# Unread matrix products in a recurrence's first turns, zeroing moved to GpSimd, and experts' first chunks put ahead of the gates' transposes

## The chip, the cores and the metric

The kernel runs on one core of a Trainium2 chip. A core has five engines that run side by side and meet at semaphores: TensorE (PE: matrix products; PEld is its weight load), VectorE (DVE), ScalarE (ACT), GpSimd (POOL) and SyncE (SP, which here only starts transfers). TensorE's clock is granted at one of two levels, 1.2 or 2.4 GHz, which the profile shows as 0.50 and 1.00. The metric is the device time of the whole program in microseconds; less is better.

## The reference

A two-layer pre-norm decoder on x and ctx_1024, each 64 sequences x 64 tokens x 128 channels in float32:

```python
x = x + attn0(layernorm(x))            # 16 heads of 8, rotary, causal
x = x + mlstm(layernorm(x), ctx, ctx)  # 4 heads of 32, below
x = x + experts(layernorm(x))          # below
x = x + attn1(layernorm(x))            # 16 heads of 8, distance bias, causal
x = x + cross(ctx, layernorm(x))       # 8 heads of 64
x = x + soft_experts(layernorm(x))     # 64 experts x 32 slots

def mlstm(q, k, v):                    # the "recurrence", in its parallel form
    gates = concat(q, k, v) @ gate_kernels + biases      # input and forget gate of 4 heads
    cs = cumsum(log_sigmoid(fg))
    log_D = where(tril, cs - cs.T, -inf) + ig.T
    max_log_D = max(log_D, -1); D = exp(log_D - max_log_D)
    C = (q @ k.T) / sqrt(32) * D
    h = (C / (maximum(abs(sum(C)), exp(-max_log_D)) + 1e-6)) @ v
    return headwise_layernorm(h) * outnorm_scale

def experts(x):                        # 1 shared of 512, 15 routed of 256
    shared = gelu(x @ sW1 + sb1) @ sW2 + sb2
    weights = softmax(x @ gW + gb)
    gated = weights where among the top 3, else 0
    routed = gelu(x @ rW1[e] + rb1[e]) @ rW2[e] + rb2[e]  # all 15, weighted by gated
    return shared + sum(gated[e] * routed[e]) + x
```

## The kernel before

The 4096 tokens are 32 tiles of 128 (NT = 32, two sequences each). x stays in SBUF through all stages; each stage leaves the normalized, transposed x (g_xnT) for the next. The stages follow one another with a barrier between them: load and norm, attention 0 (tiles at_), the recurrence (ml_), the experts (ff_), attention 1 (at_ again), cross-attention (xa_), soft experts (sm_). In a stage each engine has its own instruction stream, written out by hand as turns; every wait is a semaphore count. An engine runs its stream strictly in this order, so what stands in it behind a wait waits too.

**Attention** (`attention`, both layers): vblk holds the values spread out so that one product serves two heads; the places between the values must be zero. DVE zeroes its four buffers (L493) at the start of its stream, each with an increment of `zeroed`. ACT waits for that when it first writes each buffer (L640). In layer 0 what follows on DVE is the rotation's first products (L544) from the projections of PE (L439); then SP turns pairs by DMA (L381), and POOL sums (L572, L575) and spreads the keys (L582). In layer 1 DVE copies the projections (L554, L555) and POOL spreads the keys (L582).

**Recurrence** (`mlstm`): the gates of all tokens come first, with chains of small steps between engines. PE projects and transposes them (L723 to L731), waits for DVE's and ACT's log-sigmoid, makes the cumulative sum (L735), transposes (L737), waits for the running minimum, transposes again (L739). Then 32 turns of one tile each. In a turn PE makes the outputs of tile t-2 (L757, bank p_h), transposes a finished tile (L300), makes the values of tile t (L770, bank p_n) and the decay and scores of tile t+1 (L782, L785, L792, bank p_x, two in turn). ACT takes exponentials (L945), copies the values (L956) and splits heads (L932); DVE multiplies (L851), and with POOL normalizes the outputs of earlier tiles. L782 of a tile waits for L851 of the tile two before.

**Experts** (`experts`): eight groups of 512 tokens, in each 34 chunks of 128 hidden units (4 of the shared expert, 2 of each routed one). A chunk: three products with W1 in split float32 (L1134 to L1136, bank p_h, two in turn), Gelu on ACT (L1306), for routed chunks the product with the gate on DVE (L1240), rounding on ACT (L1317), the rest on POOL (L1081), and four chunks later three products with W2 (L1121 to L1123). Turn t also prepares group t+1: logits (L1150) at chunk 1, a router of 16 steps on DVE from chunk 4 with an exponential on ACT at chunk 7 (L1320), the rounding of x (L1288, and the remainder on DVE, L1231) at chunk 20, transposes of the gates on PE (L1155) at chunk 21, and their copy on ACT (L1325). SP stores the copy and spreads each gate over 128 partitions (L1087, L1098, five buffers). Turn -1 has no chunks and prepares group 0 in the same order: logits, router, x, transposes. In turn 0 ACT also rounds the late weights at chunks 4, 8, 12, 16, 20 and 24 (L1277), and DVE makes their remainders (L1185). ACT must load a table when it goes between Gelu and the exponential.

The lines that set the places:

```python
AT_LOGITS, AT_ROUTER, AT_G_T = 1, 4, 21
AT_X = 20
SPLIT_AT = [4, 8, 12, 16, 20, 24]
```

## Time and profile before

| | us |
|---|---|
| median of 3 runs | 2082.07 |
| the three runs | 2078.18 to 2083.69 |
| profiled execution, its own time | 2085.51 |
| its span, first to last instruction | 2083.6 |
| mean granted TensorE clock over the span | 0.965 |

All rows come from the one profiled execution. "L735" is a line of the kernel. A row of the timeline gives start, duration, engine, line, operation, the tile written <- the tiles read, the shape; in square brackets the idle time of the engine before it and who released it. A row of windows gives busy time of each engine in a stretch; its number after POOL is the granted clock. In the turns of the recurrence PE works without a pause at the low clock, then at the high one with short waits. Attention 0 lasts from about 50 to 256 us, the recurrence from 257 to 386 us, the experts from 387 to 842 us, attention 1 from there to about 1045 us.

### The profile page before, as it was taken

The page shows a single profiled execution, that of the slowest core. Times are in us where ns is not written, and L with a number is a line of the kernel's source. Part 1 is how long each engine was busy: PE and PEld are TensorE (multiplying, and loading weights), DVE is VectorE, ACT ScalarE, POOL GpSimd, SP SyncE. Part 2 cuts the span into 40 slices and gives each one's busy share as a digit, 9 for nine tenths or more (in the row PEclk, how much of TensorE's full clock was granted, in tenths as well). Part 3 has the DMA queues.
Part 4 walks back from the last instruction along what each step waited for, and adds up shares of the span by engine and source line. Part 5 has one row for each costly group of instructions (what it writes and reads, how often), then busy time and mean ns, then how long its engine had stood idle before and what let it go on. Part 6 is the DMA issues. An engine that isn't in the chain of part 4 may idle for free. (4 is left out here: it accounts for less than half of the span.)

```text
span 2083.6 us, 62428 instructions
## 1 busy us (share of the span) xinstructions
PE 1872.1 (90%) x23360; PEld 1479.8 (71%) x23422; DVE 1459.4 (70%) x3903; ACT 1449.4 (70%) x4203; POOL 1117.0 (54%) x1445
## 2 busy tenths in 40 slices
PE   5799798599999999799879999767999999999898
PEld 3566566477777777466668888646888888888787
DVE  7799748556666664577746666577777777777567
ACT  5588758488888888588858888666666666666542
POOL 5677427578888889455423333137544444445420
PEclk9999959799999999899989999998999999999999
DMA  3011010122222222000011111110000000000101
GB/s 97 27 46 41 13 32 3 48 91 72 72 77 77 77 72 66 23 2 2 2 26 33 34 34 34 47 39 4 5 15 18 6 15 5 15 15 3 55 8 39
DMA packets 60620, 72.48 MB, mean 35 GB/s; under 512 B 10264, under 2 KB 38696, under 8 KB 60064
## 3 DMA queue, kind: packets, MB, share of 16 engines
q1 hardware_dynamic: 51104, 64.29, 10.5%
q10 hardware_dynamic: 9216, 4.20, 0.7%
q8 instruction: 188, 3.08, 0.6%
q14 instruction: 112, 0.92, 0.1%
HBM read 51.43 MB, written 4.44 MB: 27 GB/s over the span
## 5 line engine op out<-in xcount | busy, mean ns | idle before, releaser
L1081 POOL TENSOR_TENSOR ff_hl<-ff_hid,ff_hh 128x512 fp32r<-128x512 f32 x272 | 349.5, 1302 | 74.5 <-ACT ff_hh L1317 65.7
L1935 POOL TENSOR_TENSOR sm_zsum<-sm_zsum,sm_logits 128x512 f32<-128x512 f32 x120 | 154.1, 1284 | 276.4 <-ACT sm_logits L1961 274.7
L1240 DVE TENSOR_TENSOR ff_hid<-ff_p_b,ff_gates 128x512 f32<-128x512 f32 x240 | 164.5, 686 | 150.0 <-ACT ff_p_b L1306 148.9
L1978 ACT ACTIVATE sm_sT<-sm_p_s 128x512 f32<-128x512 f32 x128 | 69.5, 594 | 220.8 <-PE sm_p_s L1771 220.8
L613 ACT ACTIVATE at_pr<-at_p_s,at_small 128x64 f32<-128x64 f32 x512 | 155.3, 330 | 62.7 <-DVE at_small L501 62.7
L1317 ACT ACTIVATE ff_hh<-ff_hid 128x512 fp32r<-128x512 f32 x272 | 169.9, 625 | 36.9 <-DVE ff_hid L1240 36.8
L1306 ACT ACTIVATE ff_p_b<-ff_p_h,early_b 128x512 f32<-128x512 f32 x240 | 157.0, 654 | 20.5 <-PE ff_p_h L1136 19.1
L1947 POOL TENSOR_TENSOR sm_logits<-sm_logits,sm_peak 128x512 f32<-128x512 f32 x128 | 163.1, 1295 | 13.6 <-ACT sm_comb L1996 12.9
L1785 PE MATMUL sm_p_l<-g_phi,g_xnT 128*128 128x256 f32 x512 | 143.3, 407 | 26.4 <-ACT sm_logits L2006 25.3
L582 POOL TENSOR_TENSOR at_kblk<-at_kT,early_heads 128x512 f32<-128x512 f32 x128 | 131.9, 1051 | 35.5 <-PE at_p_s L479 27.8
L1819 PE MATMUL sm_p_y<-sm_w,sm_sT 128*32 128x128 f32 x4096 | 125.4, 274 | 9.2 <-ACT sm_combT L1968 8.6
L1884 DVE TENSOR_REDUCE sm_rmax<-sm_p_l 128x2 f32<-128x512 f32 x128 | 88.3, 690 | 64.3 <-PE sm_p_l L1785 63.6
L1785 PEld LDWEIGHTS sm_p_l<-g_phi,g_xnT 128*128 128x128 f32 x512 | 91.6, 198 | 54.9 <-ACT sm_logits L2006 28.0
L1827 PE MATMUL sm_p_o<-sm_yy,sm_combT 128*64 128x129 f32 x2048 | 127.5, 276 | 1.5 <-issue 1.5
L1819 PE MATMUL sm_p_s<-sm_w,sm_sT 128*32 128x128 f32 x4096 | 124.3, 273 | 1.3 <-issue 1.3
L1819 PEld LDWEIGHTS sm_p_y<-sm_w,sm_sT 128*32 128x32 f32 x4096 | 107.6, 110 | 22.9 <-ACT sm_sT L1978 11.6
L1916 DVE TENSOR_TENSOR sm_yy<-sm_p_y,sm_wb 128x512 f32<-128x512 f32 x128 | 88.0, 691 | 50.1 <-PE sm_p_y L1819 50.1
L1134 PE MATMUL ff_p_h<-ff_xh,fw_w1h 128*128 128x512 f32 x272 | 113.8, 418 | 9.1 <-ACT ff_p_b L1306 9.0
L1827 PEld LDWEIGHTS sm_p_o<-sm_yy,sm_combT 128*64 128x64 f32 x2048 | 110.2, 136 | 15.8 <-DVE sm_yy L1916 12.5
L1585 ACT ACTIVATE xa_pr<-xa_p_s,xa_sm 128x128 f32<-128x128 f32 x256 | 91.8, 391 | 38.8 <-DVE xa_sm L1497 38.8
L281 POOL TENSOR_TENSOR xa_n_rstd<-xa_n_mv,g_eps 128x1 f32<-128x1 f32 x32 | 19.9, 620 | 177.2 <-DVE xa_n_mv L267 177.2
L1121 PE MATMUL ff_p_y<-ff_hh,fw_w2h 128*128 128x512 f32 x272 | 110.7, 407 | 4.6 <-POOL ff_hl L1081 2.4
(301 smaller groups left out, 5616.8 us busy)
## 6 DMA issues: line engine op xcount, KB each, us to landing
ff_gates<-kept_gates SPq DMA_DIRECT2D x120, 256.0 KB, 3.2
xa_kturn<-xa_ksin SPq DMA_DIRECT2D x128, 64.0 KB, 2.0
at_turned<-at_terms SPq DMA_DIRECT2D x64, 64.0 KB, 1.9
sm_w<-in_w_soft SPq DMA_DIRECT2D x8, 512.0 KB, 3.5
early_whole<-in_L_ffn_rW SPq DMA_DIRECT2D x30, 128.0 KB, 2.6
early_xs<-in_x ACTq DMA_DIRECT2D x32, 64.0 KB, 2.0
ld_ctx<-in_ctx ACTq DMA_DIRECT2D x32, 64.0 KB, 2.1
x_kept<-early_xs SPq DMA_DIRECT2D x1, 2048.0 KB, 7.4
```

What stands on the lines that cost most here:

```text
L582: op = pool.tensor_tensor(kblk[:, v % 2, b, :, :], row_bc(kT[:, v, b * S:(b + 1) * S], HH), col_bc(heads[:, :], S), ALU.mult)
L613: op = act.activation(pr[:, v, h * S:(h + 1) * S], p_s[0][:, h * S:(h + 1) * S], ACT.Exp, bias=small[:, v, 0, h:h + 1], accum_out=small[:, ...
L1081: eng.tensor_tensor(hl[:, q, :], hid[:, q, :], hh[:, q, :].bitcast(F32), ALU.subtract).then_inc(h_split, 1)
L1134: pe.matmul(p_h[n % PH][:, :], w1h[:, c, :], xh[:, u, :], start=True, stop=False)
L1240: dve.tensor_tensor(h, p_b[c % 2][:, :], gates[:, n % GR, :], ALU.mult).then_inc(scaled, 1)
L1306: act.activation(into, p_h[(NC_FF * t + c) % PH][:, :], ACT.Gelu, bias=b1[:, c:c + 1]).then_inc(gelud, 1)
L1317: act.activation(hh[:, q, :], hid[:, q, :], ACT.Copy).then_inc(h_rounded, 1)
L1785: mm = pe.matmul(p_l[h][:, a * CW:(a + 1) * CW], xnT[:, t * P:(t + 1) * P], phi[:, c % 2, :], start=True, stop=True)
L1819: mm = pe.matmul((p_y, p_s)[j % 2][a][SP * k:SP * (k + 1), (b * CQ + q) * D:(b * CQ + q + 1) * D], sT[:, j % 2, a, b, n_ * SP:(n_ + 1) * S ...
L1827: mm = pe.matmul(p_o[j % 2][b * S:(b + 1) * S, a * E1:a * E1 + D + 1], combT[:, j % RING_C, q, a, b * S:(b + 1) * S], yy[:, j % 2, a * PER ...
L1935: pool.tensor_tensor(z, z, logits[:, j % RING_L, :, :], ALU.add).then_inc(summed, 1)
L1947: pool.tensor_tensor(here, here, row_bc(peak[:, c % 2, :], TU), ALU.subtract).then_inc(centred, 1)
```

## The change

1. Attention (both layers): the four zeroings of vblk go from DVE to the head of POOL's stream.
2. Recurrence: PE makes products that nobody reads, identity times mask in bfloat16, 128x128 by 128x256 (`keep_busy`): 16 before the cumulative sum, 4 before the first transpose, 3 before the second; in turns 1 and 2 eight more at the head of the tile's values; in turns 1 to 11 four more behind the wait for the former tile's copied values. They write bank p_n, or bank p_h1 for the eights. In all 83.
3. Experts: turn -1 rounds x before the router. The transposes of group 0's gates and their copy stand behind chunk 2 of turn 0. In turn 0 what prepares group 1 (logits, router, exponential, transposes, gates' copy; not x) comes five chunks later (LATE = 5).

```diff
-            for v in range(R):
-                dve.memset(vblk[:, v, :, :, :], 0.0).then_inc(zeroed, 1)
...
         def _(pool):
+            for v in range(R):
+                pool.memset(vblk[:, v, :, :, :], 0.0).then_inc(zeroed, 1)
             at["in"].wait(pool)
...
+            def keep_busy(n, bank=p_n):
+                for _ in range(n):
+                    pe.matmul(bank[:, 0:W], identb[:, :], mask[:, :], start=True, stop=True)
+            keep_busy(16)
             pe.wait_ge(gate_step, 4)
...
+            keep_busy(4)
             pe.wait_ge(u_made, 3)
...
+            keep_busy(3)
             pe.wait_ge(max_made, 1)
...
+                    if 0 < k < 3:
+                        keep_busy(8, p_h[1])
                     if has(k - 1):
                         pe.wait_ge(v_copied, k)
+                    if 0 < k < 12:
+                        keep_busy(4)
...
-        AT_LOGITS, AT_ROUTER, AT_G_T = 1, 4, 21
+        AT_LOGITS, AT_ROUTER, AT_G_T, LATE = 1, 4, 21, 5
...
+                late = LATE if t == 0 else 0
...
-                    if c == AT_LOGITS and nxt:
+                    if c == AT_LOGITS + late and nxt:
...
-                    if c == AT_G_T and nxt:
-                        pe.wait_ge(r_step, STEPS * (t + 2))
+                    n = t if t == 0 and c == 2 else t + 1
+                    if live(n) and ((c == AT_G_T + late and t >= 0) or (n == 0 and t == 0)):
+                        pe.wait_ge(r_step, STEPS * (n + 1))
...
-                    if c == AT_X and nxt:
+                    if c == (AT_X if t >= 0 else AT_ROUTER) and nxt:
...
-                    if nxt and c >= AT_ROUTER and c - AT_ROUTER < len(router):
-                        router[c - AT_ROUTER]()
+                    if nxt and 0 <= c - AT_ROUTER - late < len(router):
+                        router[c - AT_ROUTER - late]()
...
-                    if c == 7 and nxt:
+                    if c == AT_ROUTER + 3 + late and nxt:
...
-                    if c == AT_G_T + 1 and nxt:
-                        act.wait_ge(gT_done, t + 2)
+                    n = t if t == 0 and c == 2 else t + 1
+                    if live(n) and ((c == AT_G_T + 1 + late and t >= 0) or (n == 0 and t == 0)):
+                        act.wait_ge(gT_done, n + 1)
```

PE's instructions in the recurrence, from the last transposes of the gates to the values of tile 1, before:

```order
L731 MATMUL ml_p_x<-g_ident,ml_gT 128x128 x8
L735 MATMUL ml_p_h<-ml_logf,mw_tri 128x128
L737 MATMUL ml_p_h<-g_ident,ml_nu 128x128
L739 MATMUL ml_p_h<-g_ident,ml_negM 128x128
L782 MATMUL ml_p_x<-mw_mask,mw_identb 128x256
L785 MATMUL ml_p_x<-ml_negM,ml_sel 64x64 x8
L792 MATMUL ml_p_x<-ml_q,early_ctxT 64x128 x4
L770 MATMUL ml_p_n<-mw_centre,early_ctxT 128x256
L782 MATMUL ml_p_x<-mw_mask,mw_identb 128x256
```

The same place after the change (L738 is `keep_busy`; the other lines have moved down by 7 to 13):

```order
L731 MATMUL ml_p_x<-g_ident,ml_gT 128x128 x8
L738 MATMUL ml_p_n<-mw_mask,mw_identb 128x256 x16
L742 MATMUL ml_p_h<-ml_logf,mw_tri 128x128
L738 MATMUL ml_p_n<-mw_mask,mw_identb 128x256 x4
L745 MATMUL ml_p_h<-g_ident,ml_nu 128x128
L738 MATMUL ml_p_n<-mw_mask,mw_identb 128x256 x3
L748 MATMUL ml_p_h<-g_ident,ml_negM 128x128
L795 MATMUL ml_p_x<-mw_mask,mw_identb 128x256
L798 MATMUL ml_p_x<-ml_negM,ml_sel 64x64 x8
L805 MATMUL ml_p_x<-ml_q,early_ctxT 64x128 x4
L783 MATMUL ml_p_n<-mw_centre,early_ctxT 128x256
L795 MATMUL ml_p_x<-mw_mask,mw_identb 128x256
```

Nothing else on PE changed its order here; the unread products stand before the three waits.

PE's instructions at the start of the experts, before (L1150 logits, L1155 transposes of the gates, L1134 to L1136 one chunk):

```order
L1150 MATMUL ff_p_q<-early_gw,g_xnT 128x15 x4
L1155 MATMUL ff_p_q<-g_ident,ff_sel 15x128 x4
L1134 MATMUL ff_p_h<-ff_xh,fw_w1h 128x512
L1135 MATMUL ff_p_h<-ff_xl,fw_w1h 128x512
L1136 MATMUL ff_p_h<-ff_xh,fw_w1l 128x512
```

And after (L1165 logits, L1149 to L1151 one chunk, L1171 transposes):

```order
L1165 MATMUL ff_p_q<-early_gw,g_xnT 128x15 x4
L1149 MATMUL ff_p_h<-ff_xh,fw_w1h 128x512
L1150 MATMUL ff_p_h<-ff_xl,fw_w1h 128x512
L1151 MATMUL ff_p_h<-ff_xh,fw_w1l 128x512
L1149 MATMUL ff_p_h<-ff_xh,fw_w1h 128x512
L1150 MATMUL ff_p_h<-ff_xl,fw_w1h 128x512
L1151 MATMUL ff_p_h<-ff_xh,fw_w1l 128x512
L1149 MATMUL ff_p_h<-ff_xh,fw_w1h 128x512
L1150 MATMUL ff_p_h<-ff_xl,fw_w1h 128x512
L1151 MATMUL ff_p_h<-ff_xh,fw_w1l 128x512
L1171 MATMUL ff_p_q<-g_ident,ff_sel 15x128 x4
```

Three chunks now stand in front of the transposes that wait for the router.

ACT's instructions around the exponential for group 1, before (L1306 Gelu, L1317 rounding, L1320 exponential, L1277 rounding of weights at chunk 8):

```order
L1306 ACTIVATE ff_p_b<-ff_p_h,early_b 128x512
L1317 ACTIVATE ff_hh<-ff_hid 128x512
L1320 ACT_TABLE_LOAD
L1320 ACTIVATE ff_wt<-ff_wt 128x60
L1277 ACTIVATE fw_w1h<-early_whole 128x512
L1277 ACTIVATE fw_w2h<-early_whole 128x512
L1306 ACT_TABLE_LOAD
L1306 ACTIVATE ff_p_b<-ff_p_h,early_b 128x512
```

And after (L1324 Gelu, L1335 rounding, L1338 exponential, L1294 rounding of weights, now that of chunk 12):

```order
L1294 ACTIVATE fw_w1h<-early_whole 128x512
L1294 ACTIVATE fw_w2h<-early_whole 128x512
L1324 ACTIVATE ff_p_b<-ff_p_h,early_b 128x512
L1335 ACTIVATE ff_hh<-ff_hid 128x512
L1338 ACT_TABLE_LOAD
L1338 ACTIVATE ff_wt<-ff_wt 128x60
L1324 ACT_TABLE_LOAD
L1324 ACTIVATE ff_p_b<-ff_p_h,early_b 128x512
```

One Gelu and one rounding now stand between the weights' rounding and the two table loads, and the pair has moved from chunk 7 to chunk 12.

## Rows read from the trace of the kernel before

**Rows 1.** The profile page, part 1: busy time of each engine

```profile
PE 1872.1 (90%) x23360; PEld 1479.8 (71%) x23422; DVE 1459.4 (70%) x3903; ACT 1449.4 (70%) x4203; POOL 1117.0 (54%) x1445
```

**Rows 2.** Windows: stretch, length, busy time per engine; after POOL the granted clock

```profile
264.00:268.00 4.00, 1.50 (x12) 0.83 (x8) 2.06 (x11) 1.36 (x2) 0.00 (x0) 1.00 0.83 237
272.00:310.00 38.00, 38.00 (x405) 28.01 (x406) 17.40 (x97) 21.06 (x80) 14.58 (x33) 0.50 0.01 2
320.00:370.00 50.00, 42.36 (x771) 30.99 (x765) 42.22 (x246) 38.67 (x158) 38.90 (x88) 1.00 0.01 3
410.20:419.40 9.20, 6.12 (x16) 4.85 (x16) 5.32 (x15) 7.72 (x14) 4.48 (x5) 0.63 0.43 140
```

**Rows 3.** Timeline, start of attention 0

```profile
51.34 0.64 PE L439 MATMUL at_p_qk<-g_xnT,early_wk 128*128 128x128 f32 x2
51.56 3.12 DVE L493 MEMSET at_vblk<- 128x768 f32 x4
54.60 1.00 DVE L544 SCALAR_TENSOR_TENSOR at_terms<-at_p_qk,early_cols,early_table 128x128 f32<-128x128 f32 x4
...
58.26 0.45 POOL L572 TENSOR_TENSOR at_qT<-at_terms,at_turned 128x128 f32<-128x128 f32 x1 [11.09 <-DMA at_turned<-at_terms]
```

**Rows 4.** Timeline, start of attention 1

```profile
842.79 3.12 DVE L493 MEMSET at_vblk<- 128x768 f32 x4 [1.34 <-PEq L65]
...
843.16 0.63 PE L439 MATMUL at_p_qk<-g_xnT,early_wk 128*128 128x128 f32 x2
...
846.40 4.04 POOL L582 TENSOR_TENSOR at_kblk<-at_kT,early_heads 128x512 f32<-128x512 f32 x4 [5.40 <-DVE at_kT L555]
```

**Rows 5.** Timeline, POOL: its one copy, at the recurrence's start

```profile
256.97 1.89 POOL L895 COPY ml_sel<-mw_hot 128x2048 f32<-128x2048 f32 x1 [1.59 <-POOLq L65]
```

**Rows 6.** Timeline, recurrence: the cumulative sum, products, and four of DVE's L851

```profile
269.02 0.67 PE L735 MATMUL ml_p_h<-ml_logf,mw_tri 128*128 128x128 f32 x2 [3.28 <-DVE ml_logf L828]
...
272.07 1.12 PE L785 MATMUL ml_p_x<-ml_negM,ml_sel 32*64 32x64 f32 x16
...
276.20 0.49 DVE L851 SCALAR_TENSOR_TENSOR ml_cc<-ml_p_x,ml_dd 128x128 f32<-128x128 f32 x2 [3.94 <-ACT ml_dd L945]
...
312.44 0.49 DVE L851 SCALAR_TENSOR_TENSOR ml_cc<-ml_p_x,ml_dd 128x128 f32<-128x128 f32 x2
...
364.77 0.27 PE L782 MATMUL ml_p_x<-mw_mask,mw_identb 128*128 128x256 bf16 x1 [0.79 <-DVE ml_cc L851]
...
364.97 0.68 PE L785 MATMUL ml_p_x<-ml_negM,ml_sel 32*64 32x64 f32 x16
...
372.35 0.49 DVE L851 SCALAR_TENSOR_TENSOR ml_cc<-ml_p_x,ml_dd 128x128 f32<-128x128 f32 x2
```

**Rows 7.** Timeline, experts' group 0: PE's transposes and chunks 0, 5, 10, 12, 32, 33

```profile
394.65 1.03 PE L1155 MATMUL ff_p_q<-g_ident,ff_sel 128*15 128x128 f32 x4 [4.73 <-DVE ff_sel L1220]
...
395.33 0.78 PE L1134 MATMUL ff_p_h<-ff_xh,fw_w1h 128*128 128x512 f32 x1
...
402.45 0.39 PE L1134 MATMUL ff_p_h<-ff_xh,fw_w1h 128*128 128x512 f32 x1
...
405.13 0.68 DVE L1240 TENSOR_TENSOR ff_hid<-ff_p_b,ff_gates 128x512 f32<-128x512 f32 x1
...
408.69 1.28 ACT L1320 ACT_TABLE_LOAD   x1
...
413.30 0.80 PE L1134 MATMUL ff_p_h<-ff_xh,fw_w1h 128*128 128x512 f32 x1 [3.08 <-ACT ff_p_b L1306]
...
418.58 0.63 PE L1134 MATMUL ff_p_h<-ff_xh,fw_w1h 128*128 128x512 f32 x1
...
448.49 0.39 PE L1134 MATMUL ff_p_h<-ff_xh,fw_w1h 128*128 128x512 f32 x1
449.85 0.39 PE L1134 MATMUL ff_p_h<-ff_xh,fw_w1h 128*128 128x512 f32 x1
```

**Rows 8.** Who waited for whom, PE, groups 1 to 7 (451 to 830 us): total, times, longest

```profile
PE ff_p_h L1134 <- ACT ff_p_b L1306: 5.7, 6, 1.0
```

More of the change, by code:

```diff
@@ L1221, in turn @@
                 ]
+                late = LATE if t == 0 else 0
                 for c in range(NC_FF):
@@ L1280, in turn @@
                 on, nxt, old = live(t), live(t + 1), live(t - 1)
+                late = LATE if t == 0 else 0
                 for c in range(NC_FF):
@@ L1283, in turn @@
                         round_weights(SPLIT_AT.index(c))
-                    if c == AT_X and nxt:
+                    if c == (AT_X if t >= 0 else AT_ROUTER) and nxt:
                         if live(t - 1):
```

6 lines of the change are left out of this document (3 added, 3 removed).

## The prediction

> **What bounds the kernel now.** I read the page first, for the shares: no engine is near its limit as a whole; PE is busy 90% of the span [rows 1], but busy products at the low clock count as busy too. So the next view is windows by stage, where the number to look at is the granted clock. In the recurrence, from 272 to 310 us, PE is busy 38.00 of 38.00 us at a granted clock of 0.50, 1.2 GHz. From 320 to 370 us it stands at 1.00, 2.4 GHz, and PE has 7.64 us of idle time in 50 [rows 2]. The timeline tells the rest: DVE's L851, one per tile, goes from 276.20 to 312.44 us in ten turns, 3.62 us each, and from there to 372.35 us in 21 turns, 2.853 us each [rows 6]. In the first ten turns PE at the low clock is the bound; later DVE is, since PE now waits 0.79 us for L851 [rows 6]. The clock was still 1.00 from 264 to 268 us [rows 2]; then PE stood idle 3.28 us ahead of the cumulative sum [rows 6], and after it worked at 0.50.
> At the two attentions' starts DVE is the bound: it zeroes for 3.12 us while PE's first projections are there, and what waits for DVE's next step is late by that [rows 3, 4]. In the experts PE waits 4.73 us for the router ahead of chunk 0, and 3.08 us ahead of chunk 10 for a Gelu that stands behind two table loads and the rounding of weights; from then on the clock is low again, a mean of 0.63 from 410.2 to 419.4 us [rows 2, 7].
>
> **Zeroing by GpSimd.** Layer 0: the zeroing begins at 51.56 us, and DVE's next step at 54.60 us; the projections it needs are ready at 51.98 (51.34 + 0.64) [rows 3]. Without the zeroing it starts at 52.0: 2.6 us gained. POOL idles 11.09 us before its first work at 58.26 us, which will then be at 55.7 us; so it has from about 50 us, 5.7 us, for the four. Layer 1: projections ready at 843.79 (843.16 + 0.63), DVE's next step at 845.9 (842.79 + 3.12): 2.1 us off DVE; POOL's L582 at 846.40 could come at 844.3 [rows 4]. But here the zeroing stands in front of L582 in POOL's stream, and L582 in front of the scores. Price on POOL: no row has a POOL zeroing. From below, DVE's 0.78 us each (3.12 / 4, rows 3). The nearest POOL row is a copy of 2048 elements in 1.89 us [rows 5], 0.92 ns an element, so 768 cost 0.71, four 2.8 us. From above, the two-operand L582, 8 operations of 512 elements in 4.04 us [rows 4] (merged in pairs per tile, so at most 1.01 us each), gives 1.5 us for 768 and 6.1 for four. I take 2.8 to 3.1: POOL is free at 845.9 us, L582 is there 0.5 us sooner; but PE's next projections, which waited for DVE too, gain the full 2.1, and the first scores need only the first third of L582. I put 2.0. Together **4.6 us**; with the dear price 2.0 + 0 = 2.0. The cover is POOL's idle time; ACT's wait for `zeroed` comes some 10 us later and costs nothing.
> The trace shows POOL's first copy of all, at the recurrence's start, in 1.89 us with no work of its own before it [rows 5]. The Trainium skill (GPSIMD Engine Reference, Instruction dispatch) says that the first call of a freshly loaded kernel pays a load of code of about 6 us that no row shows. The row speaks against it for the copy; no run here shows it for a zeroing. It is rival D below.
>
> **Unread products in the recurrence.** Price of one: a chunk's six products of 512 columns take 1.36 us at the high clock (449.85 - 448.49, rows 7), 0.227 each, so 256 columns 0.113 us; from above 0.20 us, from L782's start to L785's [rows 6]; double at the low clock. The 16 take 1.8 to 3.2 us of the 3.28 us idle [rows 6], the 4 and the 3 fill two waits for DVE behind it: nothing on the path if the clock is high. They fill most of the one pause after which the clock was low. If it stays high, ten turns at 2.853 us are 28.5 instead of 36.24 us: 7.7 us. The steps between the cumulative sum and the first L851 hold about 3 us of products at the low clock (L785's 1.12 us becomes 0.68, rows 6): 0.4 to 1.5 us, I take 1.0. The fours cost 0.45 us a turn against PE's mean idle time of 0.44 us (7.64 / 50 x 2.853, rows 2), so nothing; at 0.20 each 0.36 us a turn over 11 turns, 4.0 us. The eights cost 0.9 us each in turns 1 and 2, but DVE's first turns are lighter, having no tile to normalize; in ten turns at the steady pace they are counted too long. I take + 0.5 for both. Sum **9.2 us**, 4.5 to 10.5. Late next is DVE, with 42.22 of 50 us [rows 2], in a chain with POOL; it is the 2.853 us.
> The trace has PE busy without a gap for 38 us at the low clock [rows 2]. The Trainium skill (TensorE: Matmul & The Clock Gate, The HAM clock gate) says that the default state is throttled and that sustained activity releases it. The row shows that a busy PE does not release it as such, so being busy is no guarantee for the change either. By the page the eights and fours would lift a low clock at once, 2061 to 2063; by the row they might not, 2084 (rivals B and E).
>
> **Experts, group 0.** PE is free at 389.92 (394.65 - 4.73, rows 7). Three W1 products are 1.36 us at the low clock, so chunks 0 and 1 end at 392.6. Chunk 2 needs the Gelu of chunk 0, which follows the table load of 1.28 us [rows 7] behind the router's exponential: about 393.5 to 394.8. The transposes come then, as now at 394.65, and the gates' copy and its DMAs as before. Chunk 3 starts at 395.4, chunk 4 at 396.8, and after the first three W2 products chunk 5 at 399.2 instead of 402.45: 3.2 us. The first product with a gate, L1240 at 405.13, had no idle time before it [rows 7]: DVE came from the weights, so the gate had landed. If it had only just, the 3.2 us are lost.
> Moving the exponential five chunks takes the table loads away from the weights of chunk 8. From chunk 5, seven chunks at 1.36 and some 1.0 us for weights: chunk 12 starts at 409.7 instead of 418.58, in all 8.9 us earlier. Given back: chunk 12 to 33 took 31.27 us (449.85 - 418.58), 2.7 more than 21 x 1.36, ACT being full there with weights. The two loads of 1.28 us each and the exponential now fall into it, beside the weights of chunk 12. In groups 1 to 7, without weights, such a pair costs PE 0.95 us (5.7 / 6, rows 8); all of it would be 2.8. I take 1.3. Moved with it: PE's transposes to chunk 26 and ACT's copy to 27; SP's stores and spreads for group 1 queue behind that copy, but it still has seven chunks, 9.5 us, to the group's end. Sum **7.6 us**, 2.9 (3.2 lost, all given back) to 8.9.
>
> **Sum.** 4.6 + 9.2 + 7.6 = 21.4 us. Against the profiled execution's own 2085.51 us (span 2083.6) this is 2064.1; that execution is 3.4 us above the median of the runs, so against the median 2082.07 it is 2060.7, say **2061**.
>
> **Rivals.** A is this forecast. **B, the clock falls once more at the recurrence's start** and comes back after a few turns: for, 1.5 us of idle time stay behind the 16; against, 1.00 held from 320 to 370 us with short waits [rows 2]. Three turns at 3.62 + the unread products' second half: about 4 us, 2065. **C, the clock falls in the experts behind the moved table loads**: two chunks took 5.28 us instead of 2.72 there (418.58 - 413.30, rows 7): 2.6 us, 2064. For: the loads now meet the weights of chunk 12; against: in groups 1 to 7 no wait is over 1.0 us [rows 8]. **D, POOL's zeroing in layer 0 starts late or runs long**: it has 5.7 us and needs some 3; what it takes beyond that delays its first work, which feeds everything in the attention. At 5.2 us beyond the 5.7 the gain of 2.6 is an equal loss; I price the middle, 3.3 us beyond, where POOL starts at 59 us and layer 0 loses 0.7 instead of gaining 2.6: 2064. The page named above (Trainium skill, GPSIMD Engine Reference, Instruction dispatch) would give about this. **E, the change doesn't do what it says**: the clock stays low through the first ten turns as now. The 60 products in the turns then stand with no idle time to cover them (38.00 of 38.00, rows 2) at 0.227: 13.6 us more; the 16 take 3.6 us against 3.28, 0.3 more; and no 9.2: 2082.1 - 4.6 - 7.6 + 13.9 = 2084, no change. **F, slower**: as E, but the changed rhythm keeps the clock low to turn 20; ten more turns at 3.62 instead of 2.853 are 7.7 us, 2091. It decides from six such turns on. For E and F speaks only that nobody can read from a row what lifted the clock at 310 us; against both, that PE was at 1.00 right ahead of the pause that the 16 fill.
>
> **Numbers.** A 0.60, B 0.15, C 0.12, D 0.05, E 0.05, F 0.03. The range takes A with its bounds (recurrence + 1.3 or - 4.7, experts + 1.3 or - 4.7, POOL - 2.6, not all at once), B, C and D, and the 3 us by which the three runs differ: 2053 to 2072. About 0.3%, 6 us, is what a measurement here can tell from no change: faster 0.92, same 0.05, slower 0.03.
>
> **What would show it.** Right: granted clock 1.00 from 262 to 360 us; ten turns of L851 in 28 to 29 us; DVE's first step in attention 0 at 52 us and POOL's first rotation sum at 55.7; chunk 5 about 9 us after the logits' end; no low clock after the exponential of group 1. Wrong: a clock of 0.50 in the turns (B, E, F), POOL zeroings over 1.5 us each, or the first L1240 waiting for a gate's DMA.

## The result, and the profile after

| | before | after |
|---|---|---|
| median, us | 2081.04 (4 runs) | 2059.06 (4 runs) |
| the runs, us | 2078.18 to 2083.69 | 2056.88 to 2061.03 |
| after / before | | 0.9885, 95% interval 0.9866 to 0.9905 |
| profiled execution, own time (span) | 2085.51 (2083.6) | 2060.20 (2058.1) |
| mean granted clock | 0.965 | 0.978 |

The change gains 22.0 us by the medians (23.9 by the ratio, in which each run counts); the prediction said 21.4 and 2061, and gave 2053 to 2072. A second measurement of the same kernel, on another chip, gave 0.9890 (0.9875 to 0.9905). The sum was right, but not all of its terms were. This is where the two profiled executions part, at steps that both have:

| step | before | after | earlier by |
|---|---|---|---|
| DVE's first rotation product, attention 0 | 54.60 | 52.74 | 1.86 |
| first score maxima, attention 0 | 64.94 | 63.60 | 1.34 |
| first gate product of the recurrence, L723 | 259.00 | 255.60 | 3.40 |
| tile 0's decay product on DVE (L851, now L864) | 276.20 | 271.81 | 4.39 |
| the same of tile 10 | 312.44 | 299.04 | 13.40 |
| the same of tile 31 | 372.35 | 358.92 | 13.43 |
| experts' first step on DVE | 387.00 | 373.55 | 13.45 |
| experts' chunk 12 | 418.58 | 395.94 | 22.64 |
| group 1's chunk 0 | 451.21 | 433.12 | 18.09 |
| first score maxima, attention 1 | 852.91 | 833.03 | 19.88 |
| end | 2083.6 | 2058.1 | 25.5 |

The times of this table count from the program's first instruction, so they take in that the load stage ended 0.17 us later in this profile of after (DVE's copy L489 starts at 50.15 us, before at 49.98). Counted from that copy, the first rotation product comes 2.02 us earlier, the first maxima 1.51.

Some of the gains lie in unchanged code. Between attention 0's first scores and the recurrence 2.06 us are won: about 1.1 of them since the clock fell once more at 67.7 us, for 3.4 us, in the profile of before, and in this one of after it did not. In the second profile of after it fell at 67.2 us; there tile 0 came at 273.54, only 2.66 us earlier than before. The rest, some 0.9 us, goes with the moved zeroing in every profile, whatever the clock did. From the first maxima of the ninth tile to those of the last, attention 0 takes 130.87 to 130.94 us in the six profiles with DVE's zeroing and 130.39 to 130.43 in the eight with GpSimd's, 0.5 us less. The same stretch of attention 1 takes 136.75 to 137.93 us and 136.06 to 136.27, at least 0.5 us less. What in the streams does it, no run tells. The two rows of attention 0, before and after:

```profile
110.72 0.68 DVE L501 TENSOR_REDUCE at_small<-at_p_s 128x8 f32<-128x512 f32 x1
...
241.60 0.69 DVE L501 TENSOR_REDUCE at_small<-at_p_s 128x8 f32<-128x512 f32 x1
```

```profile
107.93 0.69 DVE L499 TENSOR_REDUCE at_small<-at_p_s 128x8 f32<-128x512 f32 x1
...
238.32 0.69 DVE L499 TENSOR_REDUCE at_small<-at_p_s 128x8 f32<-128x512 f32 x1
```

Counted from DVE's copy to the recurrence's first product, attention 0 takes 209.02 us before and 206.58 in the second profile of after: 2.4 us gained.

And behind attention 1's first scores nothing was changed, yet the rest took 1230.7 us before and 1225.0 after. Over the 13 profiles of this study that have the same code there, it took 1221.6 to 1230.7 us, in part by where the clock fell at the heads of cross-attention and the soft experts. In the six of them with DVE's zeroing the mean is 1228.1 us, in the seven with GpSimd's 1225.1, but the two groups overlap. So one profile's span tells a stage's gain only where the stage is read by itself.

Attention 0 and 1 after the change, POOL's and DVE's rows of the timeline (start, duration, engine, line, operation, tiles; in brackets the idle time before and who ended it). They answer to [rows 3, 4]:

```profile
50.12 2.85 POOL L562 MEMSET at_vblk<- 128x768 f32 x4 [2.77 <-POOLq L65]
56.53 0.45 POOL L572 TENSOR_TENSOR at_qT<-at_terms,at_turned 128x128 f32<-128x128 f32 x1 [3.57 <-DMA at_turned<-at_terms]
```

```profile
50.15 0.78 DVE L489 COPY at_bvb<-early_cols 128x128 f32<-128x128 f32 x1 [2.11 <-PEq L65]
51.88 0.29 DVE L491 TENSOR_TENSOR early_bo<-at_p_v,early_bo 128x128 f32<-128x128 f32 x1 [0.95 <-PE at_p_v L390]
52.74 1.12 DVE L542 SCALAR_TENSOR_TENSOR at_terms<-at_p_qk,early_cols,early_table 128x128 f32<-128x128 f32 x4 [0.56 <-PE at_p_qk L439]
```

```profile
824.54 2.77 POOL L562 MEMSET at_vblk<- 128x768 f32 x4 [1.57 <-POOLq L65]
827.28 3.04 POOL L582 TENSOR_TENSOR at_kblk<-at_kT,early_heads 128x512 f32<-128x512 f32 x3
```

The four zeroings cost POOL 2.85 and 2.77 us. In layer 0 they begin together with DVE's copy L489, and that copy takes 0.78 us. In the profile of before it took 0.23:

```profile
49.98 0.23 DVE L489 COPY at_bvb<-early_cols 128x128 f32<-128x128 f32 x1 [2.12 <-PEq L65]
```

The recurrence, PE's cumulative sum and DVE's decay products of tiles 0, 10 and 31, against [rows 6]:

```profile
265.87 0.49 PE L742 MATMUL ml_p_h<-ml_logf,mw_tri 128*128 128x128 f32 x2 [1.45 <-DVE ml_logf L841]
```

```profile
271.81 0.49 DVE L864 SCALAR_TENSOR_TENSOR ml_cc<-ml_p_x,ml_dd 128x128 f32<-128x128 f32 x2 [3.18 <-ACT ml_dd L958]
...
299.04 0.49 DVE L864 SCALAR_TENSOR_TENSOR ml_cc<-ml_p_x,ml_dd 128x128 f32<-128x128 f32 x2
...
358.92 0.49 DVE L864 SCALAR_TENSOR_TENSOR ml_cc<-ml_p_x,ml_dd 128x128 f32<-128x128 f32 x2
```

Windows of after (start:end, length, busy time and count of PE, PEld, DVE, ACT, POOL, then the granted clock, DMA share, GB/s). The recurrence, against [rows 2]:

```profile
260.00:360.00 100.00, 87.25 (x1494) 65.11 (x1486) 73.73 (x423) 72.48 (x287) 62.79 (x143) 1.00 0.06 18
```

The clock stands at 1.00 for 100 us. Ten turns take 27.23 us instead of 36.24.

The experts' group 0, PE, against [rows 7]: transposes, chunks 5, 12, 15, and group 1's chunk 0:

```profile
380.65 0.61 PE L1171 MATMUL ff_p_q<-g_ident,ff_sel 128*15 128x128 f32 x4
...
383.15 0.39 PE L1149 MATMUL ff_p_h<-ff_xh,fw_w1h 128*128 128x512 f32 x1
...
395.94 0.40 PE L1149 MATMUL ff_p_h<-ff_xh,fw_w1h 128*128 128x512 f32 x1
...
403.11 0.80 PE L1149 MATMUL ff_p_h<-ff_xh,fw_w1h 128*128 128x512 f32 x1 [2.43 <-ACT ff_p_b L1324]
...
433.12 0.39 PE L1149 MATMUL ff_p_h<-ff_xh,fw_w1h 128*128 128x512 f32 x1
```

ACT ahead of chunk 15, where the exponential now stands:

```profile
399.54 1.28 ACT L1338 ACT_TABLE_LOAD   x1
400.83 0.25 ACT L1338 ACTIVATE ff_wt<-ff_wt 128x60 f32<-128x60 f32 x1
401.10 1.28 ACT L1324 ACT_TABLE_LOAD   x1
402.40 0.66 ACT L1324 ACTIVATE ff_p_b<-ff_p_h,early_b 128x512 f32<-128x512 f32 x1
```

And the window behind this wait:

```profile
403.00:406.40 3.40, 3.29 (x8) 2.61 (x9) 2.53 (x10) 3.30 (x7) 2.72 (x3) 0.51 0.31 98
```

The transposes wait for nobody. The wait of 3.08 us ahead of chunk 10 has become one of 2.43 us ahead of chunk 15, with a low clock behind it, now for 3.4 us: a wait moved, not removed.

### The profile page after: what moved, and what is told of

It is laid out like the page before. It is cut to its first block and busy times, and to the rows that moved or that the text cites. A ratio compares the mean times of both kernels' runs of the same rounds, so it can differ in the third digit from the quotient of the medians.

```text
span 2058.1 us, 62588 instructions
## 1 busy us (share of the span) xinstructions
PE 1863.2 (91%) x23443; PEld 1475.0 (72%) x23505; DVE 1458.5 (71%) x3895; ACT 1446.9 (70%) x4203; POOL 1123.8 (55%) x1453
## 3 DMA queue, kind: packets, MB, share of 16 engines
q8 instruction: 188, 3.08, 0.6%
## 5 line engine op out<-in xcount | busy, mean ns | idle before, releaser
L1335 ACT ACTIVATE ff_hh<-ff_hid 128x512 fp32r<-128x512 f32 x272 | 169.9, 625 | 39.1 <-DVE ff_hid L1257 38.9
L1324 ACT ACTIVATE ff_p_b<-ff_p_h,early_b 128x512 f32<-128x512 f32 x240 | 156.9, 654 | 19.3 <-PE ff_p_h L1151 18.0
L1149 PE MATMUL ff_p_h<-ff_xh,fw_w1h 128*128 128x512 f32 x272 | 114.0, 419 | 10.1 <-ACT ff_p_b L1324 9.5
L1134 PE MATMUL ff_p_y<-ff_hh,fw_w2h 128*128 128x512 f32 x272 | 110.5, 406 | 4.6 <-POOL ff_hl L1094 2.2
```

What stands on the lines that cost most here:

```text
L1324: act.activation(into, p_h[(NC_FF * t + c) % PH][:, :], ACT.Gelu, bias=b1[:, c:c + 1]).then_inc(gelud, 1)
L1335: act.activation(hh[:, q, :], hid[:, q, :], ACT.Copy).then_inc(h_rounded, 1)
```

## The experiments

All were compared with the kernel before on the same chip; a gain in us is worked out from the ratio. "Stretch" numbers are differences of the steps named in the table above, each in its own profile.

**The three parts alone.** The first run has only the diff's first part:

```diff
-            for v in range(R):
-                dve.memset(vblk[:, v, :, :, :], 0.0).then_inc(zeroed, 1)
...
+            for v in range(R):
+                pool.memset(vblk[:, v, :, :, :], 0.0).then_inc(zeroed, 1)
```

> The kernel before with the four zeroings on GpSimd alone, in both layers. Theory (ledger of the two traces): layer 0's first score maxima come 1.3 us earlier (the prediction said 2.6; 0.55 of the missing part is DVE's copy L489, 0.78 instead of 0.23 us beside the zeroing), layer 1's 1.75 us earlier: together 3.1 us, 2078. In the trace: L489 at 0.78 us again, nothing changed in the recurrence (ten turns in 36 us) and in the experts. Rival (the prediction's own sum): 4.6 us, 2076.5. Rival (a gain that is only the phase of the clock after the start, since in the profile of after the clock did not fall again at 68 us): 1.4 us more in layer 0, present here too if it comes with the zeroing, absent if it was chance.

Measured: 2078.97 us (11 runs) against 2084.80, ratio 0.9977 (0.9968 to 0.9987): 4.8 us, between 2.7 and 6.7. In its profile L489 took 0.78 us again; attention 0's first maxima came at 63.81, 1.13 us earlier; from the experts' last chunk but one to attention 1's first maxima it took 25.02 us instead of 26.75, 1.73 less. The clock fell at 66.9 us as before, so that fall's absence in the first profile of after does not come with the zeroing. Up to the first maxima the trace accounts for about 3 us. Behind them it shows 0.5 us more in each attention, by the stretches named above; from the copy to the recurrence's first product it takes 206.54 us instead of 209.02. With these the trace comes to 4.8 us (2.48 in layer 0, 1.73 and 0.58 in layer 1), as the runs say.

The second has only the unread products:

```diff
+            keep_busy(16)
             pe.wait_ge(gate_step, 4)
...
+            keep_busy(4)
...
+            keep_busy(3)
...
+                    if 0 < k < 3:
+                        keep_busy(8, p_h[1])
...
+                    if 0 < k < 12:
+                        keep_busy(4)
```

> The kernel before with the 83 unread products in the recurrence alone. Theory: all of the recurrence's gain is here, 10.0 us by the two traces (1.0 at the head, 9.0 in ten turns), 2071; ten turns of L851's successor in 27 to 28 us, granted clock 1.00 from the head to the end of the turns. Rival (the clock held because the stage began in another phase, after the faster attention): the clock falls to 0.50 again ahead of the cumulative sum or in the turns, gain 0 to 2 us, 2079 to 2082.

Measured: 2070.88 us (5 runs), ratio 0.9942 (0.9929 to 0.9955): 12.1 us, 9.4 to 14.8. Its stretch from tile 0 to tile 10 is 27.23 us, the same as in after; from tile 0 to 31 it is 87.14, 9.0 less than before. The rival falls: the part works without the faster attention ahead of it.

The third has only the experts' reordering (the diff from `LATE` on):

```diff
-        AT_LOGITS, AT_ROUTER, AT_G_T = 1, 4, 21
+        AT_LOGITS, AT_ROUTER, AT_G_T, LATE = 1, 4, 21, 5
...
+                    n = t if t == 0 and c == 2 else t + 1
+                    if live(n) and ((c == AT_G_T + late and t >= 0) or (n == 0 and t == 0)):
```

> The kernel before with the experts' reordering alone. In the profile of after the experts' first group gained 9.2 us up to chunk 12 and gave 4.6 us back by its end. Theory 1 (the stage's gain is its own): 4.7 us, 2076.4; chunk 5 some 5.9 us earlier than before, two slow chunks behind the table loads at chunk 15. Theory 2 (the clock rose early in the experts, at 379 us, only because the recurrence ended at another state): chunk 5 is 3.2 us earlier, as predicted, and with 4.6 us given back the net is -1 to 2 us, 2079 to 2082.

Measured: 2081.52 us (11 runs), ratio 0.9986 (0.9975 to 0.9996): 2.9 us, 0.8 to 5.2. The two windows of its profile, experts' first step to chunk 12 and from there to group 1, then the same two of before and of after:

```profile
387.83:410.86 23.03, 21.00 (x80) 15.32 (x81) 12.34 (x34) 16.33 (x29) 11.52 (x9) 0.82 0.35 93
410.86:448.07 37.21, 32.81 (x138) 24.14 (x137) 27.62 (x51) 33.82 (x59) 30.73 (x24) 1.00 0.35 106
```

```profile
387.00:418.58 31.58, 22.44 (x80) 17.21 (x81) 14.02 (x45) 20.74 (x34) 13.03 (x10) 0.72 0.36 93
418.58:451.21 32.63, 32.09 (x138) 24.80 (x136) 25.10 (x40) 29.66 (x54) 27.83 (x22) 0.99 0.33 103
```

```profile
373.55:395.94 22.39, 19.81 (x81) 14.48 (x82) 12.35 (x34) 16.23 (x29) 11.50 (x9) 0.88 0.39 98
395.94:433.12 37.18, 33.68 (x137) 25.53 (x137) 27.37 (x51) 34.15 (x59) 30.42 (x24) 0.95 0.37 105
```

Alone the part gains 8.55 us to chunk 12 and gives 4.58 back, 3.97 net; in after 9.19 and 4.55, 4.64 net. The first theory holds for the net gain. The 0.67 us between the two fit the higher clock at the stage's start (0.88 against 0.82), which no run varied by itself. Chunk 5 comes 10.49 us behind the stage's first step, against 15.45 before and 9.60 in after, between the two theories. Now look at ACT, the fourth of the five busy times: over the whole group it works 50.4 us before, 50.2 with this part alone and 50.4 in after. The group's length is that work plus ACT's idle time, which fell from 13.8 to 10.1 and 9.2 us. In after's second window ACT is busy 34.15 of 37.18 us, 4.49 us more than before, and the window is 4.55 us longer. PE and DVE wait there for ACT's Gelu (2.9 and 7.5 us); ACT's own waits are of at most 0.56 us each. This part alone has the clock at 1.00 through that window and needs the same 37.21 us, so it is not the clock. ACT bounds the window.

**Which half of the reordering?** The kernel before with the later preparation alone:

```diff
-        AT_LOGITS, AT_ROUTER, AT_G_T = 1, 4, 21
+        AT_LOGITS, AT_ROUTER, AT_G_T, LATE = 1, 4, 21, 5
...
+                    n = t + 1
+                    if live(n) and c == AT_G_T + late:
```

> The kernel before with LATE = 5 alone (what prepares group 1 comes five chunks later in turn 0); x, router and transposes of group 0 stay in their old order. Theory 1 (from the two traces: the wait behind the table loads only moves): chunks 5 to 12 are 3.4 us faster, chunks 12 to 34 4.6 us slower, net -1.2 us in the stage; total 2084 to 2087 against 2084.8. Theory 2 (the prediction's sum: 5.7 us gained up to chunk 12, 1.3 given back): 4.4 us, 2080.4.

Measured: 2081.48 us (11 runs), ratio 0.9988 (0.9980 to 0.9997): 2.5 us, 0.6 to 4.2. Its windows:

```profile
386.53:412.85 26.32, 20.20 (x80) 15.52 (x81) 12.31 (x34) 16.41 (x29) 11.66 (x9) 0.75 0.31 92
...
412.85:450.01 37.16, 33.76 (x137) 25.62 (x137) 27.37 (x51) 34.27 (x59) 30.34 (x24) 0.95 0.37 99
```

Up to chunk 12 it gains 5.26 us, near theory 2's 5.7, and then it gives 4.53 back, near theory 1's 4.6: net 0.73 us. Each theory had one half. Taken from the whole part's 3.97 us, the other half, x rounded before the router and the chunks put ahead of the transposes, is worth 3.24. This split rests on one profile each; the runs (2.5 and 2.9 us) can't tell the half from the whole.

**Does the place of the exponential count?** After, with another number:

```diff
-        AT_LOGITS, AT_ROUTER, AT_G_T, LATE = 1, 4, 21, 5
+        AT_LOGITS, AT_ROUTER, AT_G_T, LATE = 1, 4, 21, 2
```

> The kernel after with LATE = 2 instead of 5: logits of group 1 behind chunk 3, the exponential at chunk 9 instead of 12, behind the weights of chunk 8. Theory 1 (ScalarE is the bound of group 0's chunks; where its two table loads stand only moves the wait): group 0 from the stage's first step to group 1's chunk 0 takes 59.6 us as with 5, within 0.5 us; total as after. Theory 2 (the place counts): the loads meet the weights as before the change, chunk 12 comes 3 to 5 us later and little is won back: 2 to 4 us slower than after.

Measured: 2063.16 us (4 runs), ratio 0.9894 (0.9881 to 0.9908), the same as after. The windows:

```profile
375.63:400.89 25.26, 19.95 (x80) 14.33 (x81) 13.16 (x37) 19.15 (x32) 12.10 (x9) 0.88 0.43 109
400.89:435.74 34.85, 33.15 (x136) 25.86 (x137) 27.99 (x48) 31.17 (x56) 29.52 (x23) 0.95 0.32 102
```

Chunk 12 is 2.9 us later in the stage than in after and the rest 2.3 us shorter; the group takes 60.11 us against 59.57 and 59.64 in the two profiles of after. The 2.8 us of table loads and exponential go from one window to the other with ACT's busy time (19.15 + 31.17 = 50.3), and the group is 0.5 us longer: nearly nothing, as theory 1 says.

**The head's products without those in the turns, and the other way round.** The first kernel has only the 16, the 4 and the 3:

```diff
+            keep_busy(16)
             pe.wait_ge(gate_step, 4)
...
+            keep_busy(4)
...
+            keep_busy(3)
```

> The kernel before with only the 16, 4 and 3 unread products ahead of the cumulative sum and the two transposes; none in the turns. Theory 1 (the one pause of 3.28 us is what cost the clock): the clock stays at 1.00 through the turns, gain 8.5 to 10 us, 2071 to 2072.5, like all 83. Theory 2 (the products in the turns are needed, since the first turns are light and full of waits at the high clock): the clock falls to 0.50 in the first turns, most of the ten turns at 3.62 us, gain 0 to 3 us, 2078 to 2081.

Measured: 2076.75 us (12 runs), ratio 0.9972 (0.9957 to 0.9987), 5.8 us; but the runs go from 2071.4 to 2085.9, while those with all 83 lie between 2070.2 and 2072.6. Windows of its profile: just after the head, the turns behind, and the later turns; below them the place of after that answers to the first:

```profile
271.00:276.50 5.50, 4.18 (x60) 2.54 (x58) 1.34 (x5) 3.33 (x10) 0.00 (x0) 1.00 0.00 0
...
277.00:296.00 19.00, 19.00 (x215) 14.75 (x214) 9.05 (x51) 10.28 (x41) 7.67 (x18) 0.50 0.01 2
300.00:355.00 55.00, 47.73 (x881) 35.40 (x878) 46.49 (x272) 44.33 (x181) 42.63 (x96) 1.00 0.01 3
```

```profile
267.40:272.90 5.50, 5.16 (x70) 3.49 (x69) 1.33 (x5) 3.33 (x11) 0.00 (x0) 1.00 0.00 0
```

The head got through at 1.00 and the clock fell in the first turns, where PE was busy 4.18 of 5.50 us; with the eights and fours it is busy 5.16 there, and the clock stayed. Once fallen, it stayed low for some 20 us with PE busy all the time. Theory 1 is refuted; theory 2 is right in kind, but its 0 to 3 us are too few, since some runs keep most of the gain. The four fastest, up to 2074.0 us, have a mean clock of 0.972 to 0.975, like the runs with all 83 (0.973 to 0.974); the five slowest, from 2080.3 us, have 0.966 to 0.968.

The second kernel has only the products in the turns:

```diff
+                    if 0 < k < 3:
+                        keep_busy(8, p_h[1])
...
+                    if 0 < k < 12:
+                        keep_busy(4)
```

> The kernel before with only the unread products in the turns (eights in turns 1 and 2, fours in turns 1 to 11); none at the head. Theory 1 (two doors: the pause at the head must be filled, and the light first turns too): the clock falls ahead of the cumulative sum as before and stays at 0.50 for 20 to 41 us with PE full; the products in those turns have no cover at 0.227 us each, so the first ten turns take 36 to 48 us, total 2083 to 2098, no gain or slower. Theory 2 (the denser turns lift a low clock soon): low for under 10 us after the head, gain 5 to 8 us, 2077 to 2080.

Measured: 2075.79 us (5 runs from 2074.4 to 2076.2), ratio 0.9958 (0.9944 to 0.9971): 8.8 us. Windows:

```profile
270.00:280.00 10.00, 8.71 (x68) 5.50 (x69) 2.51 (x10) 4.65 (x15) 0.00 (x0) 0.50 0.07 20
281.00:350.00 69.00, 63.05 (x1144) 48.43 (x1142) 54.14 (x314) 54.20 (x222) 49.24 (x112) 1.00 0.01 3
```

The clock falls at the head as before, at 270.1 us, and is back at 280.3, in turn 1 behind its first twelve unread products: 10.2 us later instead of 41. These twelve stand at the low clock and do cost something, since tile 2 comes 4.13 us behind tile 1 instead of 2.89. Theory 2 holds, with a gain a little above its 5 to 8 us; the trace shows 6.7 of it from tile 0 to tile 31 (89.49 us instead of 96.16). Before, PE was busy 38.00 of 38.00 us at 0.50 and the clock did not come back [rows 2]; here unread products were put between the same products, and it did. What in them does it, no run tells.

**The price of an unread product.**

```diff
                     if 0 < k < 12:
-                        keep_busy(4)
+                        keep_busy(4 if k < 3 else 8)
```

> The kernel after with eight unread products instead of four in turns 3 to 11 of the recurrence. Theory 1 (in these turns PE's work with the four fills 2.69 us of a turn, read from the distance of two neighbouring groups of four at 291.45 and 294.14 us, and DVE's chain 2.85): with eight it is 2.69 + 0.45 = 3.14 us, PE becomes the bound and nine turns take 0.29 us more each, 2.6 us in all. Theory 2 (the idle time of 0.44 us a turn is wholly used by the four, as the prediction reckoned): 0.45 x 9 = 4.0 us. Theory 3 (unread products are always hidden): 0.

Measured: 2063.49 us (5 runs from 2060.0 to 2070.4), ratio 0.9900 (0.9883 to 0.9917), not to be told from after's. The trace is clear; PE's groups of eight, one a turn:

```profile
297.93 1.04 PE L738 MATMUL ml_p_n<-mw_mask,mw_identb 128*128 128x256 bf16 x8
301.06 1.04 PE L738 MATMUL ml_p_n<-mw_mask,mw_identb 128*128 128x256 bf16 x8
304.20 1.04 PE L738 MATMUL ml_p_n<-mw_mask,mw_identb 128*128 128x256 bf16 x8
```

A turn takes 3.13 us, as the first theory's 3.14. From tile 0 to tile 31 it is 89.60 us against 87.11 and 87.25: 2.4 us. So the fours leave 2.85 - 2.69 = 0.16 us of a turn, not nothing. The first theory holds.

**DVE's slow copy.** In layer 0 the zeroing waits for the copy:

```diff
+            if rope:
+                pool.wait_ge(bv_spread, 1)
             for v in range(R):
                 pool.memset(vblk[:, v, :, :, :], 0.0).then_inc(zeroed, 1)
```

> The kernel after, but in layer 0 GpSimd begins its zeroing only when DVE's copy L489 is done. Theory (the copy took 0.78 instead of 0.23 us because the zeroing ran beside it): the copy takes 0.23 us again, and L491 and all behind it come 0.5 to 0.6 us earlier; the zeroing then lies beside L491 and the first L542, which are operations with an operand in PSUM and keep their durations; first score maxima at about 63.0 instead of 63.60 us. Total 0.5 us better than after, below what the runs can tell. Rival (the copy is slow for another reason): 0.78 us stays, L491 no earlier.

Measured: 2061.17 us (4 runs), ratio 0.9887 (0.9874 to 0.9901), as after. DVE's rows:

```profile
50.65 0.23 DVE L489 COPY at_bvb<-early_cols 128x128 f32<-128x128 f32 x1 [2.11 <-PEq L65]
51.82 0.29 DVE L491 TENSOR_TENSOR early_bo<-at_p_v,early_bo 128x128 f32<-128x128 f32 x1 [0.95 <-PE at_p_v L390]
52.68 1.13 DVE L542 SCALAR_TENSOR_TENSOR at_terms<-at_p_qk,early_cols,early_table 128x128 f32<-128x128 f32 x4 [0.56 <-PE at_p_qk L439]
```

The copy takes 0.23 us again, and L542 comes 2.03 us behind its start instead of 2.59. So the zeroing beside the copy was the cause of its 0.78 us. The load stage ended 0.5 us later in this profile, so the scores' 63.54 by itself tells nothing. Counted from the copy they come after 12.89 us instead of 13.45; but in the run with eight unread products a turn, whose copy is slow, it is 12.94. So it isn't shown that the faster copy brings the scores forward.

**Filling more idle time.** Could the falls at the other stages' heads be filled as well? Two tries. The first, with `unread` for products of 512 columns of the experts' operands:

```diff
+                    if t > NT:
+                        keep_busy(3 if t < NT + 2 else 14, p_x[:, 0, 0, :])
                     norm.pe_transpose(pe, t - 6, t % 2, p_n[:, 2 * P:3 * P])
...
             for t in range(first, last):
                 turn(t)
+            keep_busy(12, p_x[:, 0, 0, :])
...
+                        if t == 0 and c == 15:
+                            pe.wait_ge(r_step, STEPS + 1)
+                            unread(p_q, u, 10)
...
+                        if not on:
+                            unread(p_h[0], (u - 1) % R, 10 if q == 0 else 2)
```

> The kernel after, with the zeroing held as in the run hold_zero, and unread products in four more idle stretches of PE: in the recurrence's last turns ahead of each transpose (14 each) and at its end (12), in the experts ahead of chunk 15 of group 0 (10 of 512 columns, in the wait behind the table loads), and in the experts' last turn ahead of the transposes (3, 10, 2, 2, 2). Theory 1 (what falls behind each idle stretch is the clock, and work behind it runs at 0.50): clock 1.00 from the recurrence to attention 1's start; experts' start 1.3 to 2.5 us, chunks 15 and 16 1.2 us, attention 1's start 0.5 to 2 us, the copy 0.5: 3.5 to 6 us less than after, ratio to before 0.985 to 0.987. Theory 2 (in those stretches other engines are the bound and the low clock costs nothing, or the products delay the transposes): within 1 us of after.

Measured: 2060.74 us (4 runs), ratio 0.9887 (0.9874 to 0.9901), the same as the run with the held zeroing alone. Its second window of group 0:

```profile
397.27:434.48 37.21, 35.09 (x147) 26.02 (x147) 27.61 (x51) 33.82 (x59) 30.69 (x24) 1.00 0.37 105
```

The clock no longer falls behind chunk 15 (1.00 instead of 0.95), and the window is as long as ever: 37.21 us. The low clock behind the moved loads costs nothing. From the last tile's decay product to the experts' first step it took 15.47 us instead of 14.63; the next try leaves out the 12 products at the recurrence's end and takes 14.51. From group 1 to attention 1's first maxima it took 397.96 us instead of 399.91, 2.0 us less. The group itself was 0.5 us longer. What is left by the trace, some 0.6 us, is less than the runs can tell. Theory 1's 0.985 to 0.987 is missed, and theory 2 holds.

The second try leaves out what did nothing, and adds products of identity and identity at more heads and ends:

```diff
+            unread_ident(pe, p_n, g, 9)
             pe.wait_ge(gw_summed, 2)
...
+            unread_ident(pe, pj[0], g, 14)
             pe.wait_ge(w_split, 2)
...
+                    if k >= NT - 2:
+                        pe.wait_ge(pt_copied, 2 * NT)
+                        unread_ident(pe, p_s[0], g, 4 if k == NT - 2 else 7)
```

> As the run filled, but without the products that did nothing (chunk 15) or delayed the next stage (the last 12 of the recurrence), and with unread products in more idle stretches: identity times identity in float32 ahead of the last two transposes of both attentions (4 and 7), at the head of the recurrence (9) and of cross-attention (14), and ahead of cross-attention's last transpose (10); experts' last turn 2, 8, 2, 2, 2. Theory 1 (work behind such stretches at 0.50 is on the path at the heads of stages): attention 1's start 2.0 us as in filled, the recurrence's head 0.5 to 1, cross-attention's and soft experts' heads 0.5 to 2 each: 3 to 7 us less than after. Theory 2 (only attention 1's start is worth anything, 2.0 us, the rest is hidden by other engines): 1.5 to 2.5 us less than after.

Measured: 2063.10 us (4 runs from 2058.1 to 2067.6), ratio 0.9895 (0.9877 to 0.9912). Windows of its recurrence:

```profile
260.00:267.00 7.00, 4.98 (x43) 3.15 (x36) 3.81 (x17) 3.08 (x7) 0.00 (x0) 1.00 0.63 184
267.50:277.00 9.50, 9.50 (x72) 5.89 (x72) 1.63 (x7) 4.32 (x14) 0.00 (x0) 0.50 0.07 20
```

Both theories miss: the clock now fell at 267.3 us, behind the cumulative sum, and stayed low for 10.2 us although all 83 products stand there and PE's idle time ahead of that sum is 1.45 us as in after. Tile 0 to tile 31 took 90.30 us, 3.2 more. So the 83 products hold the clock in seven profiles of eight, and are no guarantee. The gains at the heads of attention 1 (0.6 us) and cross-attention (0.9) don't pay for it. No version is faster than the kernel after by more than the runs can tell.

**Do the parts add up?** The kernel after once more:

> The kernel after once more, on the chip of the following kernels, so that they can be compared with it: ratio to before 0.9866 to 0.9905 as at first. Theory 1 (the three parts add up without helping one another): 4.8 + 12.1 + 2.9 = 19.8 us by their own runs, ratio 0.9905. Theory 2 (they help one another, since the experts' start found a higher clock behind the faster recurrence): 21 to 24 us, ratio 0.9885 to 0.990.

Measured: 2062.21 us (4 runs) against 2084.54, ratio 0.9890 (0.9875 to 0.9905): 22.9 us (19.8 to 26.1), against a sum of 19.8 by the three parts' own runs, each known to some 2 us. So the runs can't tell whether the parts help one another: theory 2's figure came, but theory 1 isn't excluded. The traces show 0.67 us of help, in the experts' start.

## Why the prediction was right, step by step

- **What bounds the kernel: right.** Clock in the recurrence's first ten turns, DVE at the attentions' starts.
- **Zeroing, layer 0: the size nearly right, the step not.** Forecast 2.6 us at DVE's first rotation product and passed on whole. Counted from DVE's copy, the trace shows 2.02 there and 1.51 at the first maxima (1.65 with this part alone). By the recurrence's first product it is 2.4 to 2.5, but 0.5 of that comes in later tiles, from something the prediction did not name: in part luck. The step that failed is "Without the zeroing it starts at 52.0": it took the projections' time as fixed, but DVE's copy L489, which they follow, became 0.55 us longer beside POOL's zeroing (0.78 against 0.23, and 0.23 when held apart). The Trainium skill (GPSIMD Engine Reference, Specifications) says that GpSimd shares its SBUF interfaces with VectorE, with contention for those of DVE's instructions that run in a 2-port perf mode or have two SBUF inputs. The trace agrees as far as it goes: the slow copy runs from SBUF to SBUF, though no row shows its mode, while DVE's copy from PSUM beside the zeroing in layer 1 was no slower (0.28 us, before 0.27 and 0.28). I had not asked what else DVE does in those microseconds.
- **Its price on POOL: right.** 2.8 us reckoned from a copy, 2.85 and 2.77 measured. Rival D did not happen: the first zeroing was there as quickly as the others. The load of code of about 6 us, which the Trainium skill (GPSIMD Engine Reference, Instruction dispatch) states for the first call of a freshly loaded kernel, does not show for the zeroing in this trace.
- **Layer 1: right**, 2.0 forecast, 1.75 in three profiles, and some 0.6 more in later tiles that was not forecast.
- **Unread products: right, for a reason half seen.** Ten turns were to take 28.5 us and took 27.23; the head 1.0 and it was 1.0 (4.39 - 3.40); together 10.0 against 9.2 (12.1 by the runs with this part alone, not under 9.4). But the prediction credited the filled pause, and took the eights and fours as cost only. The runs show that each of the two groups alone already gives 5.8 and 8.8 us, that the head alone is unsure, and that those in the turns bring back a clock that has fallen. Rival B, a clock that falls once more in the head, came in neither profile of after, but it did in the second try at filling, with all 83 products in place: even all 83 do not exclude it. Rivals E and F rested on "The 60 products in the turns then stand with no idle time to cover them": true of the first twelve in the run without the head's products, which cost 1.2 us, and refuted for the others, since the clock did not stay low.
- **The weighed rule.** By the Trainium skill (TensorE: Matmul & The Clock Gate, The HAM clock gate) activity releases the throttled state. From it I had worked out that the turns' products would lift a low clock at once; the row of 38.00 busy us at 0.50 spoke against it. The run without the head's products sides with the rule for this kind of product: the clock was back behind the first twelve of them, 10.2 us after its fall. The row still stands for the kernel's own products.
- **Experts ahead of chunk 12: right**, 8.9 us forecast, 9.19 measured; the chunks put ahead 3.2 forecast, 3.24 measured. But the way there was another, and that the sum fits is luck. Up to chunk 5 the stage gained 5.85 us (9.60 from its first step, before 15.45) where 3.2 were forecast, and from chunk 5 to 12 it gained 3.34 (12.79, before 16.13) where 5.7 were. The clock rose at 379 us, ahead of chunk 2, earlier than reckoned; DVE's first product with a gate waited 1.70 us.
- **Given back: the term that was mis-sized.** 1.3 us forecast, 4.55 measured. The step was the cost of "such a pair" taken from groups 1 to 7, where ACT has no weights to round. From chunk 12 on ACT is the bound (34.15 of 37.18 us), so the whole of its 2.8 us counts, and another 1.7 us: one Gelu and one rounding that ran ahead of chunk 12 before (1.3 us), and what crosses the window's edge. I had written "ACT being full there with weights" and not drawn the consequence. The later preparation as a whole, 4.4 us in my sum, is worth 0.73 in the trace of that half alone.
- **Rival C happened**, a fall behind the moved loads for 3.4 us, and cost nothing instead of its 2.6 us: with the clock held at 1.00 the window stayed 37.21 us.
- **The sum.** By the traces the steps that the forecast counted give 3.1 + 10.0 + 4.6 = 17.7 us where 21.4 was forecast; the runs say 22.0 and 22.9. That the forecast came out so near is in part luck: 4 us and more of the measured gain do not lie in those steps. Some 1.7 us of it are what the moved zeroing gives later in the two attentions (4.8 us in all instead of 3.1), in every profile. The rest, 2.6 us and more, is open. Some of it can be the clock's course in unchanged code (1221.6 to 1230.7 us behind attention 1's first scores, before at the upper end); whether the change favours that course, or the profiles show it by chance, the runs don't tell.

## What to carry to other kernels

Read a stage by the engine that is nearly full in it (here ACT, 34.15 of 37.18 us) and that the others wait for: a step moved along a full engine's stream moves the wait and gains little (0.73 of the 4.4 us forecast), and a term "given back" must be priced on that engine, not on the one that waits. Unread products in idle time are cheap as long as a turn has room (0.11 us each here), but put them where work behind is bound by PE; the low clock beside ACT's bound cost nothing. When work goes from DVE to GpSimd, ask which of DVE's operations run beside it. And count a stage from its own start in both profiles: the load stage alone ended up to 0.8 us later in one profile than in another.

## What the runs showed of the hardware

- A DVE copy of 128x128 float32 within SBUF took 0.23 us alone and 0.78 us beside a GpSimd zeroing, in every profile (0.23 again when the zeroing was held).
- Four GpSimd zeroings of 128x768 float32 in a row took 2.77 to 2.85 us, 0.69 to 0.71 each; DVE needed 3.12 [rows 3].
- Fallen to 0.50 in the recurrence, the clock stayed low for 37.5 to 44.4 us in the four profiles without unread products, for 20.5 with those at the head alone, and for 10.2 in the two in which it fell with those in the turns in place.
- With unread products at attention 0's end and nine at the recurrence's head, the clock no longer fell at some 252 to 256 us, but at 267.3, with the same 83 products there.
